# First cross-attention of a perceiver kernel: weights of later stages requested in two parcels, behind the refills of turns 1 and 2

## What is computed

```python
# 16 heads of 8 features; query = layernorm(x), key = value = context
q = split_heads(query @ Wq + bq)
k = split_heads(key @ Wk + bk)
v = split_heads(value @ Wv + bv)
logits = einsum('bhqd,bhkd->bhqk', q, k) / sqrt(DH) + mask * -1e9
attn = softmax(logits)
out = einsum('bhqk,bhkd->bhqd', attn, v) @ Wo + bo
# the stage after it (L0_attn): Wk and Wv are 128 x 64, 8 heads of 8,
# and each key and value head serves two query heads
k4 = repeat(k.reshape(B, S, 8, 8), 2, axis=2)
v4 = repeat(v.reshape(B, S, 8, 8), 2, axis=2)
```

## Time and profile before

| | us |
|---|---|
| median of 3 runs | 1418.92 |
| lowest and highest run | 1415.0 and 1423.77 |
| the profiled execution | 1424.09 |
| its span | 1422.3 |

### The profile page before, as it was taken

The page is one execution under the profiler, slowest core; times in us unless marked ns, Lnnn a source line. Parts: engine busy times, 40 slices in busy tenths (PEclk is TensorE's granted clock), DMA queues, the critical chain, the costliest instruction groups (busy, mean ns, idle before and its releaser), DMA issues. The chain is left out here.

```text
span 1422.3 us, 40223 instructions
## 1 busy us (share of the span) xinstructions
PE 1212.9 (85%) x14789; PEld 901.4 (63%) x14790; DVE 845.9 (59%) x3051; ACT 729.0 (51%) x1582; POOL 315.9 (22%) x687
## 2 busy tenths in 40 slices
PE   5799999866776899999977999999999996668655
PEld 2577777636654577777746888888888873213333
DVE  3477777657844356655545555555555554563587
ACT  2477777537832345444434655555555555425333
POOL 1122221145400111111102444444444440000000
PEclk8899999989956899999989999999999999778855
DMA  2432333100000523333203554545454440000001
GB/s 77 107 74 73 74 74 74 31 1 1 0 0 5 175 83 86 101 89 89 60 8 110 136 133 120 134 119 134 120 133 120 133 112 1 0 0 1 22 0 30
DMA packets 93270, 100.96 MB, mean 71 GB/s; under 512 B 17240, under 2 KB 82400, under 8 KB 93024
## 3 DMA queue, kind: packets, MB, share of 16 engines
q1 hardware_dynamic: 93152, 99.37, 26.4%
HBM read 87.59 MB, written 11.74 MB: 70 GB/s over the span
## 5 line engine op out<-in xcount | busy, mean ns | idle before, releaser
L1377 POOL TENSOR_TENSOR d_p<-d_p,d_rtotal 128x289 f32<-128x289 f32 x256 | 170.3, 665 | 246.5 <-DVE d_rtotal L1517 246.5
L1511 DVE CUSTOM_DVE_ANT_0 d_p<-bank,d_low 128x289 f32<-128x289 f32 x256 | 112.4, 439 | 180.6 <-PE bank L1406 180.6
L1476 ACT ACTIVATE d_p<-d_p,d_nmax 128x289 f32<-128x289 f32 x256 | 137.6, 538 | 98.8 <-DVE d_nmax L1511 98.7
L1419 PE MATMUL bank<-d_pT,d_xr 32*128 32x128 f32 x5120 | 160.9, 275 | 0.0
L1406 PE MATMUL bank<-x_keyT,d_q 128*128 128x289 f32 x512 | 154.8, 423 | 2.5 <-DVE d_nmax L1511 1.3
L1419 PEld LDWEIGHTS bank<-d_pT,d_xr 32*128 32x128 f32 x5120 | 148.7, 187 | 8.8 <-issue 1.5
L430 ACT ACTIVATE a_p<-a_p,a_nmax 128x257 f32<-128x257 f32 x256 | 109.4, 499 | 75.9 <-DVE a_nmax L463 75.9
L1141 PEld LDWEIGHTS bank<-c_w,c_hs 128*128 128x128 f32 x1024 | 120.9, 194 | 14.8 <-issue 14.8
L1525 DVE STREAM_TRANSPOSE d_pT<-d_p 128x320 f32<-128x320 f32 x256 | 128.5, 502 | 1.1 <-POOL d_p L1377 1.1
L1132 PE MATMUL bank<-yT,c_w 128*128 128x512 f32 x256 | 117.6, 603 | 4.6 <-DMA c_w<-in_L_ffn_w 4.6
L1141 PE MATMUL bank<-c_w,c_hs 128*128 128x128 f32 x1024 | 121.1, 277 | 0.0
(11 more groups left out here) (261 smaller groups left out, 2132.3 us busy)
## 6 DMA issues: line engine op xcount, KB each, us to landing
d_xr<-key_rows SPq DMA_DIRECT2D x256, 160.0 KB, 3.1
d_low<-mask_low SPq DMA_DIRECT2D x64, 144.5 KB, 3.4
a_ctT<-in_ctxT SPq DMA_DIRECT2D x64, 128.5 KB, 2.1
a_low<-mask_low SPq DMA_DIRECT2D x64, 128.5 KB, 3.1
c_ct<-in_ctx SPq DMA_DIRECT2D x64, 128.0 KB, 2.3
key_rows<-c_ct SPq DMA_DIRECT2D x128, 64.0 KB, 2.0
c_w<-in_L_ffn_w SPq DMA_DIRECT2D x8, 514.0 KB, 4.3
xT<-in_xT SPq DMA_DIRECT2D x4, 256.0 KB, 3.6
```

The source lines that it names most:

```text
L1377: nc.gpsimd.tensor_tensor(p, p, rtotal[:, b % 2, g:g + 1].broadcast_to([128, KEYS]), ALU.mult).then_inc(normed, 1)
L1419: ins = nc.tensor.matmul(O[j], xr[rows, b % 2, k, :], pT[rows, b % 2, :, 32 * k:32 * k + 32], start=(k == 0), stop=(k == BLOCKS - 1))
L1476: nc.scalar.activation(p, p, ACT.Exp, bias=nmax[:, b % 2, g:g + 1], scale=-1.0, accum_out=total[:, b % 2, g:g + 1]).then_inc(exp_made, 1)
L1511: nc.vector.tensor_tensor_reduce(P[:, b % 2, g, 0:KEYS], S[u % 2], low[:, b % 4, :], -1.0, 3.4e38, ALU.add, ALU.min, accum_out=nmax[:, b % ...
```

## The change

On SP's queue in the loop's block:

- The loads of turn 1 (elements 4 to 7, each a `ctT` and a `low` request with their waits) come right after the four requests of `vlast`.
- Then come the weights of `L0_attn`, as `load_b` of its own, then the loads of turn 2 (elements 8 to 11), then the remaining eleven requests of `load_rest`, then the loop over turns 3 to 15. Turns 1 and 2 are unrolled.
- `Wk` and `Wv` of `L0_attn` come from the host already doubled, 128 x 128 each (`np.repeat` of the heads' columns), and are loaded with one plain request each in place of two with 32-byte runs. `load_b` so has eight requests in place of nine, three of 64 KB among them, and the counts waited for fall from 160 to 128.

```diff
-    def load_rest(self, sp, t):
+    def load_b(self, sp, t):
         sp.wait_ge(self.zeroed, 1)
-        sp.dma_start(self.b["wq"][:], t["L0_attn_Wq"]).then_inc(self.b_loaded, 16)
-        for dst, name in ((self.b["wk"], "L0_attn_Wk"), (self.b["wv"], "L0_attn_Wv")):
-            for r in range(2):
-                sp.dma_start(dst[:].rearrange("p (n r d) -> p n r d", r=2, d=8)[:, :, r, :],
-                             t[name].rearrange("p (n d) -> p n d", d=8)).then_inc(self.b_loaded, 16)
+        for n, name in (("wq", "Wq"), ("wk", "Wk"), ("wv", "Wv")):
+            sp.dma_start(self.b[n][:], t[f"L0_attn_{name}"]).then_inc(self.b_loaded, 16)
         for r in range(2):
             rows = slice(64 * r, 64 * r + 64)
             sp.dma_start(self.b["mem"][rows, rows], t["L0_attn_memory"]).then_inc(self.b_loaded, 16)
             sp.dma_start(self.b["norm_col"][rows, :], t["L0_attn_memory_norm"]).then_inc(self.b_loaded, 16)
         sp.dma_start(self.b["gate"][:, 0:1], t["L0_attn_memory_weight"].broadcast_to([128, 1])).then_inc(self.b_loaded, 16)
+
+    def load_rest(self, sp, t):
         sp.dma_start(self.c["router"][:], t["L0_ffn_router_w"]).then_inc(self.rest_loaded, 16)
...
+                for r in range(RING):
+                    load(1, r)
+                w.load_b(sp, t)
+                for r in range(RING):
+                    load(2, r)
                 w.load_rest(sp, t)
-                with sp.Fori(1, QUADS) as i:
+                with sp.Fori(3, QUADS) as i:
                     for r in range(RING):
                         load(i, r)
...
-                pe.wait_ge(w_loaded, 160)
+                pe.wait_ge(w_loaded, 128)
...
-    for n in ("Wq", "Wk", "Wv", "memory"):
+    for n in ("Wq", "memory"):
         put[f"L0_attn_{n}"] = a[f"L0_attn_{n}"]
+    for n in ("Wk", "Wv"):
+        put[f"L0_attn_{n}"] = np.repeat(a[f"L0_attn_{n}"].reshape(D, 8, 1, 8), 2, axis=2).reshape(D, D)
```

More of the change, by code:

```diff
@@ L125, in wait @@
     def wait(self, sp):
-        for loaded, count in ((self.a_loaded, 128), (self.b_loaded, 160), (self.rest_loaded, 176)):
+        for loaded, count in ((self.a_loaded, 128), (self.b_loaded, 128), (self.rest_loaded, 176)):
             sp.wait_ge(loaded, count)
@@ L591, in _ @@
                 nc.vector.memset(gate[:, 1:2], 0.0).then_inc(gate_step, 1)
-                dve.wait_ge(w_loaded, 160)
+                dve.wait_ge(w_loaded, 128)
                 dve.wait_ge(gate_step, 2)
@@ L610, in _ @@
             def _(act):
-                act.wait_ge(w_loaded, 160)
+                act.wait_ge(w_loaded, 128)
                 act.wait_ge(gate_step, 2)
```

## The result

The changed kernel takes 1410.47 us in the median of 20 runs (1404.29 to 1416.94), the kernel before 1420.45 (20 runs, 1415.0 to 1426.69). The ratio is 0.9938, 95% interval 0.9921 to 0.9955: 8.8 us less, between 6.4 and 11.2. 8.15 us had been forecast, and 1410.8 for the time.

The account below looks back on a forecast made before the run. The steady loop waits on TensorE's scores, its start on a late `ctT` refill behind 20 SP requests. Part 1's 8.15 us, other parts 0, off 1424.09 gave 1415.9, less 5.2 for the median 1410.8; range 1404.5 to 1417.5.

Parts of the forecast that it names:

- Part 1: First cross-attention loop, elements 3 to 6: refills of turn 1 ahead of weights remove the 6.3 us `ctT` wait; gain 8.15 us.
- Part 2: `load_b` behind turn 1's refills: holds SP 3.7 to 5.5 us, element 8's refill still lands in time; cost 0.
- cover: Time left between a refill's landing behind a parcel and TensorE's need: 2.7 us at element 8, 2.5 at element 12.
- Part 3: Remaining eleven `load_rest` requests behind turn 2's refills: element 12's refill is 2.6 us late but lands in time; cost 0.
- Part 4: Doubled Wk and Wv: four 32-byte-run requests become two plain ones; no second gain, and 0 taken for an earlier `vlast`.
- second case: Rival before element 2: `vlast` lands earlier without the small runs; gain 8.15 plus up to 2.3 us, 1408.5; chance 0.12.
- bound of 0.9 us late: Most that `vlast` could be delayed by refills following it: 0.3 us for 65 KB plus 0.6 for half a refill.
- The stall only partly gone: Rival: one parcel outlasts its cover, TensorE waits 2.4 us and restarts slowly; 3.8 us of gain left, 1415.1; chance 0.13.
- the stall coming back twice: Rival: both parcels hold their refills, TensorE idles at elements 8 and 12, 8.3 us each; 1427.4 us; chance 0.04.
- restart at half clock: TensorE resuming at lowered clock after idling for a late refill: 2.0 us on top of the wait.

Follow-up runs that it names:

- e2: Kernel before with only the host-doubled Wk and Wv, one plain request each, requests in the old order; ratio to the kernel before 0.9947.
- e3: Changed kernel with both groups of weight requests issued as one of 19, behind the refills of turn 1; ratio to the kernel before 1.0004.
- e1: Changed kernel with Wk and Wv loaded in the old form, two loads each in 32-byte runs; ratio to the kernel before 0.9963.

## Why the prediction was right

- **The number** is nearer than the working. 1410.8 was forecast and 1410.47 measured, but the base of three runs, 1418.92, lay 1.5 us below the 1420.45 of twenty, and the medians of twenty differ by 10.0 us and not by 8.15. The errors of 1.5 and 1.8 us cancel, which is luck. The size of the gain, 8.5 us by the traces and 8.8 by the ratio, is what the working got right to within 0.7.
- **Part 1** held. First refill requested at 33.32 in a loop that began 1.5 us earlier; no wait for `ctT`; element 4 at 51.52 for 51.6 forecast, element 6 at 58.51 for 58.77, element 63 at 262.47 for 262.7 (with the 1.5 us of the earlier start made up by chance, as said above). The gain of elements 3 to 6 is 18.89 - 10.42 = 8.47 us for 8.15. The refill of element 4, asked for right behind `vlast`, took 6.9 us to land and not 3.2; it was there at 40.2, still some 8 us before TensorE wanted it. The small error is in the pace: I took 3.58 us for each of elements 4 to 6 and put the 6.99 us that the old run needed from 4 to 6 down to catching up after the stall. The changed kernel needs 6.99 there as well (51.52 to 58.51), without a stall.
- **Part 2** held: parcel of 5.0 us at SP (51.31 to 56.29) for 3.7 to 5.5, the next refill at 56.29 for 56.9, cover 3.7 us (2.9 in the second profile) for 2.7. Behind it the queue was not as smooth as drawn, two mask requests held SP for 1.2 and 1.7 us; this cost nothing.
- **Part 3** held: 65.55 to 71.4 for 66.0 to 71.1; the refill at 72.19 for 71.1, a microsecond later, and 4.1 us to landing for 3.56. Of the cover of 2.5 us 0.9 was left, 1.2 in the second profile: this parcel, and not the first, is the one that nearly cost something. In 70 to 80 us no engine waits for a transfer.
- **Part 4** was right in taking 0 for the earlier `vlast`: from the first request to the first edge product it takes 8.4 to 9.3 us in all profiles with the full read, with the small runs behind it (8.67, 8.89), the refills (8.43, 9.26), or the plain weights (8.60). The forecast's second case, an earlier `vlast`, is thereby out. The read-modify-write rule of the Trainium skill ("DMA: Bandwidth & Descriptors", section "Specifications") was quoted for it: whatever transfers under 512 bytes cost, it wasn't `vlast` that paid. The ring order that the Trainium skill states in the section "Queues, rings and completion order" of the same page was quoted too, and the trace agrees: the refill asked for behind `vlast` landed at 40.2, just after the first edge product began at 39.97. (The bound of 0.9 us late in the forecast is too wide: half a refill at 226 GB/s is 0.3 us and not 0.6. Nothing hangs on it.) But I said of part 4 only that it isn't a second gain. e2 shows more: alone it was the whole one in that profile. The rows would have shown most of it: the four requests in small runs hold SP from 35.1 to 41.5, two plain ones of 0.46 take 0.9, so the refill goes out 5.5 us earlier, of a wait of 6.3. The other 1.0 us came from the small requests behind them, which were quicker in e2 (3.1 us for the five, for 4.15).
- **The rivals.** The stall only partly gone and the stall coming back twice both failed in this kernel, but e3 shows that the mechanism is real: one parcel of 12.6 us costs 5.9 us, and e1, with one of 7.4 us, has the first trace of it. The price I gave for the restart at half clock, 2.0 us, was 1.0 in e3.
- **What was not in the sum.** In the first profile after, elements 0 to 3 took 15.27 us against 13.67, with the clock at 0.50 until 46 us and 0.73 to 49. In the eight profiles with the full `vlast` read this interval lies between 12.4 and 15.3 us, in both orders, and it too goes with the clock: 0.52 were granted in it in the two longest (15.3 in the changed kernel, 15.1 in e2), 0.68 to 0.71 in the other six. Why the clock differs between executions isn't shown.

## What to carry to other kernels

Where one queue issues both the refills of a ring and loads for later stages, work out for each refill when its slot is free, when it is wanted and how long it takes to land; the loads that fit into the rest are free, in parcels, and what goes beyond it is paid in full, with a restart at half clock on top (1.0 and 2.2 us in the two stalls here). Leave a margin: the same refill took 2.7 to 4.3 us to land. Before adding up two fixes of one wait, take each alone: a wait can only be removed once. And compare two profiles by the intervals that the change can reach; the rest of the span can differ by as much as the effect without any cause in the change, and the clock granted in a stretch tells where to look.

## What the runs showed of the hardware beyond that

In two of nine profiles one instruction of VectorE in the memory attention, a 128x512 multiplication from and to SBUF (line 791) that otherwise takes 0.69 us and at most 1.0, took 3.8 us. The line's own view of the kernel before, then GpSimd's instructions in that time (count, busy us and mean ns, idle us before):

```profile
L791 DVE TENSOR_TENSOR b_p<-b_p,b_rtotal x16: 691/692/3824, 317.6 to 390.6; 128x512 f32<-128x512 f32 x16
```
```profile
L646 POOL TENSOR_TENSOR b_qb<-b_qT,b_own_head 128x128 f32<-128x128 f32 x5 | 2.0, 399 | 0.0
L645 POOL TENSOR_TENSOR b_kb<-b_kT,b_key_scale 128x128 f32<-128x128 f32 x5 | 2.0, 398 | 0.0
```

And the same line in the changed kernel:

```profile
L795 DVE TENSOR_TENSOR b_p<-b_p,b_rtotal x16: 691/692/987, 306.1 to 374.9; 128x512 f32<-128x512 f32 x16
```

GpSimd ran ten multiplications without a pause while VectorE's one was held. In the changed kernel the two meet too, and there both give way: VectorE's instruction takes 0.97 us, and GpSimd's next one 0.79 in place of 0.40. The Trainium skill, "SBUF — State Buffer", section "SBUF: two separate sides", describes a port pair that VectorE, in an instruction with two inputs in SBUF like this one, shares with GpSimd: the one that starts first blocks the other for the whole instruction. The 0.97 us fit that, with a wait shorter than one of GpSimd's instructions; the 3.82 us don't, with VectorE held over about eight. No run here tests whether the ports are the cause. The two profiles with this instruction, 3.82 and 3.86 us, are the two whose memory attention took 75 us.

A second observation: the same request doesn't always hold SP equally long. A pair of 32-byte-run loads held it 5.07 us behind `vlast` and 1.64 us in e1, and plain requests that usually take 0.33 to 0.43 us took up to 1.7 in the parcels and among the refills right behind them. What it depends on wasn't varied further: in the slow case 1 MB of `vlast` had just been asked for, and plain requests at that place (e2) took 0.43 to 0.46.
